# Round 2 of a graph network: chain and assembling ahead of a variance on VectorE

## What is computed

```python
for _ in range(num_rounds):                      # 4 rounds
    h = x @ W
    msgs = h[src] * norm[:, None]
    agg = jax.ops.segment_sum(msgs, dst, num_segments=n) + b
    mu = agg.mean(axis=-1, keepdims=True)
    var = agg.var(axis=-1, keepdims=True)
    x = (agg - mu) * jax.lax.rsqrt(var + EPS) * gamma + beta
```

## Time and profile before

| | us |
|---|---|
| median of 3 runs | 11049.81 (11042.33 to 11066.14) |
| the profiled execution, its own time | 11056.49 |
| its span | 11054.7 |
| busy in the span: POOL, DVE, PE, ACT | 7208.5, 6769.6, 5819.0, 2887.5 |
| mean granted TensorE clock | 0.68 of full speed |

### The profile page before, as it was taken

The page is one execution under the profiler, slowest core; times in us unless marked ns, Lnnn a source line. Parts: engine busy times, 40 slices in busy tenths (PEclk is TensorE's granted clock), DMA queues, the critical chain, the costliest instruction groups (busy, mean ns, idle before and its releaser), DMA issues. The chain is left out here.

```text
span 11054.7 us, 113652 instructions
## 1 busy us (share of the span) xinstructions
PE 5819.0 (53%) x26903; PEld 4127.3 (37%) x26903; DVE 6769.6 (61%) x14006; ACT 2887.5 (26%) x5217; POOL 7208.5 (65%) x7087
## 2 busy tenths in 40 slices
PE   3757999100000004666777776767674558722255
PEld 2352333000000004665556565555553447622234
DVE  8953332595878785665767665878775766511127
ACT  0042222001222223333434443222221322100045
POOL 3755777587777776444767665767777767677720
PEclk9978999555555555666877777777776665555578
DMA  0073333163545453224766565655444999611158
GB/s 14 7 252 101 71 72 71 42 201 104 165 148 165 148 165 95 81 84 123 217 200 222 189 203 178 222 192 152 131 136 126 316 249 121 95 47 46 46 186 244
DMA packets 1454720, 1555.31 MB, mean 141 GB/s; under 512 B 1037506, under 2 KB 1158688, under 8 KB 1454491
## 3 DMA queue, kind: packets, MB, share of 16 engines
q1 hardware_dynamic: 1191816, 1284.78, 36.7%
q0 software_dynamic: 252160, 248.38, 12.3%
q10 hardware_dynamic: 10514, 19.71, 0.5%
HBM read 883.57 MB, written 800.52 MB: 152 GB/s over the span
## 5 line engine op out<-in xcount | busy, mean ns | idle before, releaser
L2601 POOL DMA_INDIRECT r_got<-state,comb_src x1176 | 1183.2, 1006 | 432.5 <-issue 344.3
L312 POOL DMA_INDIRECT payload_or_bias_rows<-payload,place x784 | 907.4, 1157 | 483.5 <-issue 254.3
L1446 POOL DMA_INDIRECT hop_got<-edges_b,next_col x784 | 808.6, 1031 | 537.4 <-ACT hop_got L1684 278.5
L1796 PE MATMUL hop_ps_into<-hop_out,span_s 128*128 128x256 f32 x8 | 4.9, 713 | 2050.4 <-DVE hop_out L1620 2050.4
L1446 POOL DMA_INDIRECT hop_got<-edges_a,next_col x784 | 782.3, 998 | 259.5 <-issue 238.4
L1796 PEld LDWEIGHTS hop_ps_into<-hop_out,span_s 128*128 128x128 f32 x8 | 2.0, 312 | 2052.7 <-DVE hop_out L1620 2052.7
L1684 ACT COPY hop_got<-hop_zeros 128x1792 f32<-128x1792 f32 x224 | 377.4, 1685 | 1206.1 <-DVE hop_ps_msg L1571 1099.9
L1620 DVE SCALAR_TENSOR_TENSOR hop_out<-hop_out,hop_runs_now,hop_ps_msg 128x256 f32<-128x256 f32 x1176 | 565.5, 481 | 50.9
L2881 PE MATMUL r_ps_v<-dense1g,r_gt 128*128 128x128 f32 x3136 | 586.6, 360 | 0.0
L2881 PEld LDWEIGHTS r_ps_v<-dense1g,r_gt 128*128 128x128 f32 x3136 | 532.3, 263 | 133.0 <-issue 133.0
L2701 DVE SCALAR_TENSOR_TENSOR r_acc<-r_acc,r_runs_now,r_got 128x64 f32<-128x64 f32 x1173 | 334.8, 285 | 272.7 <-DMA r_got<-state,comb_src 229.6
(11 more groups left out here) (816 smaller groups left out, 17998.6 us busy)
## 6 DMA issues: line engine op xcount, KB each, us to landing
edges_a<-hop_out SPq DMA_DIRECT2D x112, 896.0 KB
edges_b<-hop_out SPq DMA_DIRECT2D x112, 896.0 KB, 4.3
r_in<-state SPq DMA_DIRECT2D x168, 448.0 KB
hop_side<-x_dst SPq DMA_DIRECT2D x280, 224.0 KB, 4.2
own<-plain_y SPq DMA_DIRECT2D x56, 952.0 KB
x_and_sums<-c_y SPq DMA_DIRECT2D x56, 896.0 KB
bn_in<-x_and_sums SPq DMA_DIRECT2D x56, 896.0 KB
r1a_in<-own SPq DMA_DIRECT2D x84, 448.0 KB
```

The source lines that it names most:

```text
L312: nc.gpsimd.indirect_dma_start(out=t.raw[:, n, :], out_offset=None, in_=t.pay[k], in_offset=bass.IndirectOffsetOnAxis(t.place[:, k, n:n + ...
L1446: pool.indirect_dma_start(out=got[:, u, c, :], out_offset=None, in_=table, in_offset=at, bounds_check=EP - 1, oob_is_err=False).then_inc(g ...
L2601: pool.indirect_dma_start(out=got[:, n, c - b * CT, :], out_offset=None, in_=table, in_offset=bass.IndirectOffsetOnAxis(idx[:, at + c:at + ...
```

## The change

```diff
             def _(ago):
                 order_of_work = ((NORM, variance), (JOIN, r_variance), (0, front), (JOIN, r_norm), (NORM, norm))
+                if keeps:
+                    order_of_work = ((0, front), (NORM, variance), (NORM, norm))
                 for lag, work in order_of_work:
                     for i, u in ago(lag):
                         work(i, u)
```

## The result

The changed kernel takes **10977.53 us** (median of 4 runs, 10967.5 to 10990.33) against 11046.18 us before (median of 4, 11042.33 to 11066.14): ratio 0.9934, interval 0.9922 to 0.9947. The forecast was 10970, range 10947 to 11003. The profiled execution took 10974.5 us, its span 10972.7, 82.0 less than before.

The account below looks back on a forecast made before the run. A ring of waits through PE, ACT and DVE was taken to bound round 2; 27 periods cut from 22.47 to 19.5 us save 80 us, 11056.5 to 10976, less 6.7 to the median: 10970 us, range 10947 to 11003.

Parts of the forecast that it names:

- The ring: Round 2: assembling, transposes, products of s and t, square and variance of t, chain, next assembling; sets the 22.47 us period.
- POOL at 18.94 us stays just under that: Round 2: POOL's own pace for a chunk of 14 gathers, 18.94 us, claimed to stay below the new 19.5 us period.
- The ring's term: Round 2 period in the new order: 19.27 us short, 21.63 us long, taken as 19.5 us on average.
- Roots: DVE's waits for roots of t and n0, no longer covered by a piece of chain: 0.51 us each.
- DVE's own limit: Shortest round 2 period that DVE's work allows, should PE be faster: 18.86 us.
- one long period in ten: Round 2: share of 21.63 us periods at PE's lower clock, against about 27% before; gives 19.5 us.
- POOL's term: Round 2: POOL's busy time plus issue before gathers, 18.94 us a chunk, including 1.5 us of delays.
- the second rival: Round 2: POOL sets the pace, each wide DVE write delaying a gather; 21.5 us period, 26 us gained, 11024; chance 0.08.
- The cited rule: SBUF contention in round 2: the trace was read as agreeing for DVE's wide writes, not for the chain.
- the estimate of 4 us a chunk: Round 2: extra hold on POOL if the 14 chain instructions, 0.30 us each, also blocked gathers.
- Costed at nothing: Round 2: SP's later stores of t and loads of the next n0, put at nothing; other stretches expected as before.
- The signs named ahead: Round 2: expected assembling spacing, POOL, `gx`, square and root waits, and clock above 0.77; gathers over 1.2 us would refute.

Follow-up runs that it names:

- the thinned kernel: Changed kernel with 5 instead of 7 gathers in each half chunk of round 2, missing rows zero: period 17.66 us, total 10919.24 us.
- The filled wait: Kernel before, with 18 unread identity transposes on PE ahead of its wait for `gx` in round 2: period 20.72 us, total 10990.09 us.

## Why the prediction was right, and where it wasn't

**The ring.** Right as to what it was: it set the pace before (22.35 us with POOL thinned out), it is the wait that the new order cuts, and it gave way to each edit that shortened it.

**"POOL at 18.94 us stays just under that."** This step failed. Two terms were mis-sized: with POOL out of the way the new order runs at 17.66 us, where 19.5 was forecast, and POOL takes 19.40, where 18.94 was. That the second error put the period within 0.03 us of the forecast is luck; the bound that the forecast named, the ring, was not the one that held.

**The ring's term.** Three parts were too dear. Roots were put at 0.51 us each; they cost 34.0 / 112 = 0.30, so they doubled in number and hardly in sum. DVE's own limit, 18.86 us, was walked with those roots and with the old order's gaps; the thinned kernel ran a mean of 17.66. And the clock: I took one long period in ten, with a short one at 0.83; in the thinned kernel the clock between the assemblings is 0.92, and the squares keep DVE waiting for 5.4 us in the whole round. The filled wait shows that the clock alone is worth at least 22.47 - 20.72 = 1.75 us a period in the old order. In the changed kernel itself PE still stands 3.1 us for `gx` ((92.8 - 8.6) / 27; I said 2 to 3), and the clock is 0.84. POOL's lateness is some 0.6 of that: in the thinned kernel PE stands 2.5 us.

**POOL's term, and the second rival.** The rival's condition came true and its price did not. Counted as said next, 129 of the 140 wide writes of round 2 meet a gather. But the 0.81 us of the earlier trace rows was among the dearest cases, a gather begun 0.16 us into the write. Grouped by what DVE was at 0.13 us after their start, those beside a scaling of n0, n1 or s last 1349 ns on average (79), beside the scaling of t 1402 (26), beside the assembling 1339 (24); beside the chain 949, beside nothing 944. That is some 0.41 us each and 129 x 0.41 / 28 = 1.9 a chunk: 14 x 1.245 + 1.9 = 19.3. The 18.94 was a mean over periods in which POOL often stood still while DVE wrote; a freed POOL is met more often: 81 writes before by the same count, at 1.5 us a chunk, and 129 now, at 1.9. The bound had to be priced at the new state, with the mean case.

**The cited rule.** The Trainium skill (SBUF — State Buffer, Who interferes with whom) has a VectorE instruction with two SBUF inputs contend with a GpSimd instruction that reads SBUF. The runs agree for the 128x896 writes (scaled from the copy 1097 ns a gather, from PSUM 965). I read the chain as an exception to it, from one gather that began between two chain instructions (that of 6259.31); this reading was wrong. In the changed kernel's round 2 a gather takes 0.944 us alone, and one that is held ends 0.82 us behind the DVE instruction that it began in. So it loses what is left of that instruction less some 0.13 us. All 24 gathers begun inside an assembling and 103 of the 104 begun inside a scaling come out within 0.01 us of that (nothing, where less is left). Of the 70 begun inside a chain instruction of 0.285 us, the 14 with 0.14 to 0.17 us of it left took 958 to 984 ns, the 50 with up to 0.104 us left took at most 947, and the six begun in its first 0.03 us were not held. By these numbers a chain instruction can take at most 0.285 - 0.13 = 0.16 us from a gather; it took 5 ns on average, and the estimate of 4 us a chunk did not come.

**Costed at nothing, and rightly:** the loads (PE waited 10.9 us for them, 9.7 of it the start) and the other rounds. The signs named ahead: assemblings 19 to 20 us apart, POOL's wait near nothing, the squares under a third (29.7 of 137.2), the clock above 0.77 (0.82), gathers under 1.2 us held; PE's 2 to 3 us and the doubled roots did not.

**Open:** how much of the assembling's hold could go, since no kernel here reads `gx`'s inputs from PSUM; and why a gather begun in the first 0.03 us of a chain instruction is not held.

## What to carry to other kernels

Where a ring of waits is cut, work out the next engine's pace anew at the state after: a pace read while that engine was being held back can be too good (18.94 us read, 19.40 run). To learn which of two bounds sets a period, thin out the suspected engine's work: the ring of before kept its 22.35 us, the changed kernel fell to 17.66. And a reorder that moves work out of an idle wait only pays where the wait is on the ring; in a round that already runs at the gathers' pace it can put other work behind a late gather, 10 us here.

## What the runs showed that I had not expected

Idle transposes in PE's wait made round 2 of the kernel before 52 us shorter, by 486 added instructions between the assemblings (3024 against 2538) and a granted clock of 0.87 in place of 0.78. And what holds a gather in round 2 is a DVE instruction with both inputs in SBUF: a gather begun inside one ends about 0.82 us behind its end, so a write of 1.09 us can cost it up to 0.8 us and a chain instruction a few hundredths. Beside scalings of the same 1.09 us that read PSUM the median is 944 ns and the longest 947.
